# Score matmuls moved to the end of TensorE's attention step, with three moves on ScalarE and GpSimd that go with them

## The reference

```python
x = x + attn(layernorm(x))        # below
x = x + ffn(layernorm(x))         # top 4 of 32 experts per token, swiglu, plus a shared swiglu

def attn(X, Wq, Wv, q_norm_w, v_norm_w):
    K = X.reshape(B, L, H, d)
    Q = rms_norm_multihead((X @ Wq.T).reshape(B, L, H, d), q_norm_w)
    V = rms_norm_multihead((X @ Wv.T).reshape(B, L, H, d), v_norm_w)
    W = cumsum(einsum('blhd,blhe->blhde', K, V), axis=1)
    return einsum('blhd,blhde->blhe', Q, W).reshape(B, L, D)
```

## Time and profile before

| what | value |
|---|---|
| device time, median of 3 runs | 561.97 us (561.77 to 563.79) |
| profiled execution, its own time | 559.33 us |
| its span | 557.4 us |
| TensorE busy | 527.4 us (95%) |
| VectorE busy | 382.2 us (69%) |
| ScalarE busy | 376.5 us (68%) |
| GpSimd busy | 331.8 us (60%) |
| mean granted clock of TensorE | 0.983 |

### The profile page before, as it was taken

One profiled execution on the slowest core, in us unless ns is written; L12 is line 12 of the kernel. 1 busy time (PEld: TensorE's weight loads), 2 busy tenths in 40 slices (PEclk: granted clock), 3 DMA queues, 4 the chain that ended last, 5 costly groups with the idle time before them and its releaser, 6 DMA issues.

```text
span 557.4 us, 18176 instructions
## 1 busy us (share of the span) xinstructions
PE 527.4 (95%) x5177; PEld 383.1 (69%) x5177; DVE 382.2 (69%) x1354; ACT 376.5 (68%) x1258; POOL 331.8 (60%) x367
## 2 busy tenths in 40 slices
PE   6798999999999999699999999999999999997996
PEld 2355666666666665357998988999999995544554
DVE  7698999999999996664444444444444446744786
ACT  2687899988989985402766766777677776653452
POOL 6010377776777777771665555666666564446992
PEclk8999999999999999899999999999999999998999
DMA  8998355556456554954676776766666554428999
GB/s 259 316 292 264 125 217 211 187 215 227 186 198 246 188 192 152 366 194 127 195 219 201 221 225 199 214 193 194 194 193 198 180 187 145 143 79 342 408 409 347
DMA packets 65088, 123.29 MB, mean 221 GB/s; under 512 B 9824, under 2 KB 44000, under 8 KB 64992
## 3 DMA queue, kind: packets, MB, share of 16 engines
q1 hardware_dynamic: 47824, 78.07, 44.1%
q0 software_dynamic: 13056, 39.86, 19.2%
q10 hardware_dynamic: 4112, 4.19, 2.3%
HBM read 58.49 MB, written 63.60 MB: 219 GB/s over the span
## 4 chain that ended last, share of the span: by engine, by line
PE 79%; DMA 5%; DVE 4%; issue 4%; ACT 3%; POOL 2%; SPq 1%; ACTq 1%; DVEq 0%; POOLq 0%
PE pS L967 18%; PE pQV L828 10%; PE pS L985 9%; PE pS L741 8%; PE pS L795 5%; PE pO L888 5%; DMA xg<-xs 3%; PE pO L869 3%; PE pT L946 3%; PE pQV L946 2%; PE pQV L757 2%; PE pO L757 2%; PE pT L774 2%; PE pO L803 2%; PE pT L817 1%
## 5 line engine op out<-in xcount | busy, mean ns | idle before, releaser
L495 POOL DMA_INDIRECT ys<-gsh,dst x144 | 138.1, 959 | 108.3 <-ACT gsh L663 86.6
L467 POOL DMA_INDIRECT xs<-xg,posi x128 | 123.8, 967 | 52.1 <-issue 31.4
L967 PE MATMUL pS<-after_a,x2T_all 128*128 128x128 f32 x1024 | 135.5, 276 | 0.0
L967 PEld LDWEIGHTS pS<-after_a,x2T_all 128*128 128x128 f32 x1024 | 124.5, 192 | 0.0
L1375 DVE TENSOR_TENSOR after_a<-after_a,pS 128x128 f32<-128x128 f32 x144 | 41.5, 288 | 79.9 <-ACT after_a L651 76.1
L1346 DVE COPY x2T_all<-w 128x512 f32 x144 | 63.9, 444 | 32.9 <-issue 32.5
L985 PE MATMUL pS<-w,after_a 128*128 x256 | 76.7, 381 | 0.0
L1089 DVE TENSOR_TENSOR w<-pS,tri 128x512 f32<-128x512 f32 x96 | 65.1, 679 | 1.0 <-PE pS L795 1.0
L828 PE MATMUL pQV<-w 128*128 128x512 f32 x128 | 63.7, 621 | 0.5 <-ACT w L533 0.5
L663 ACT ACTIVATE gsh<-pS,xg 128x256 f32<-128x256 f32 x128 | 60.6, 474 | 0.4 <-issue 0.4
L662 ACT CAST dst<-xg 128x1 int32 x128 | 24.5, 191 | 45.3 <-PE pS L985 43.3
(11 more groups left out here) (221 smaller groups left out, 1019.8 us busy)
## 6 DMA issues: line engine op xcount, KB each, us to landing
xg<-xs SPq DMA_DIRECT2D x128, 160.0 KB, 2.8
ys<-gsh SPq DMA_DIRECT2D x32, 512.0 KB
w<-ys SPq DMA_DIRECT2D x32, 512.0 KB, 15.3
w<-in_L_ffn_W ACTq DMA_DIRECT2D x1, 4096.0 KB, 18.6
out<-xall SPq DMA_DIRECT2D x14, 256.0 KB, 7.2
xs<-padrow SPq DMA_DIRECT2D x32, 80.0 KB
xg<-xs SPq DMA_DIRECT2D x32, 80.0 KB, 2.2
ys<-gsh,dst POOLq DMA_INDIRECT x144
```

The lines of the kernel that those rows point to most:

```text
L467: pool.indirect_dma_start(out=xs, out_offset=bass.IndirectOffsetOnAxis(ap=posi[:, a.r8, k:k + 1], axis=0), in_=xr[:, a.r8, :], in_offset=N ...
L495: pool.indirect_dma_start(out=ys, out_offset=bass.IndirectOffsetOnAxis(ap=dst[:, j % 8:j % 8 + 1], axis=0), in_=y[:, j % 8, :], in_offset= ...
L967: last = pe.matmul(pS[a.b][:, n * P:(n + 1) * P], w13_staged(a.t)[:, (2 * k + n) * F:(2 * k + n + 1) * F], xgT[:, a.b, k, :], start=(k == ...
```

## The change

Four moves, no work added or removed. TensorE's scores of a tile go from the front of step t+2 (between L785 and L803) to the end of step t+1 (behind L888). ScalarE's copy of the scores goes to the front of its step. GpSimd's mask goes from behind the second scatter of a tile to behind the first. ScalarE's exponential for the Newton guess goes ahead of the router's L597.

```diff
@@ GpSimd
                     scatter(a, 0)
-                if (a := tile_of(9)) is not None:
-                    scatter(a, 1)
                 if (a := tile_of(2)) is not None:
                     pool_wait(S["s_copied"], banks_copied(a.t) + 1)
...
                                        pattern=[[0, 4], [1, P]], channel_multiplier=-1).then_inc(S["masked_pool"], 1)
+                if (a := tile_of(9)) is not None:
+                    scatter(a, 1)
@@ ScalarE
             def step(tile_of):
+                if (a := tile_of(3)) is not None:
+                    copy_scores(a, 1)
                 if (a := tile_of(1)) is not None:
                     wait(act, S["xnT_ps"], a.t + 1)
...
-                if (a := tile_of(3)) is not None:
-                    copy_scores(a, 1)
                 if (a := tile_of(2)) is not None:
                     wait(act, S["qT_ps"], a.t + 1)
...
-                if (a := closing(tile_of(7))) is not None:
-                    wait(act, S["max_done"], 2 * a.p + 2)
-                    act.activation(nmx[:, a.pb, :], m8[:, :, 0], ACT.Copy, scale=-1.0).then_inc(S["nmx_done"], 1)
                 if (a := tile_of(1, LAG)) is not None:
...
                     act.activation(guess[:, first:NR], lnm[:, first:NR], ACT.Exp, scale=-0.5).then_inc(S["guess_done"], 1)
+                if (a := closing(tile_of(7))) is not None:
+                    wait(act, S["max_done"], 2 * a.p + 2)
+                    act.activation(nmx[:, a.pb, :], m8[:, :, 0], ACT.Copy, scale=-1.0).then_inc(S["nmx_done"], 1)
@@ TensorE
-                if (a := tile_of(2)) is not None:
...
                     last.then_inc(S["o_ps"], 1)
+                if (a := tile_of(1)) is not None:
+                    if a.t == 0:
+                        pe.wait_ge(S["consts_dve"], DVE_CONSTS)
+                    wait(pe, S["qm_done"], a.t + 1)
+                    wait(pe, S["masked"], banks_masked(a.t))
+                    wait(pe, S["s_copied"], banks_copied(a.t))
+                    for g in range(KC):
+                        for j in range(4):
+                            last = pe.matmul(pS[j][:, g * 256:(g + 1) * 256], xnT[32 * j:32 * j + 32, a.r3, g, :],
+                                             qm[32 * j:32 * j + 32, :, g, :], start=(g == 0), stop=True,
+                                             skip_group_check=True)
+                            if g == KC - 1:
+                                last.then_inc(S["scores_ps"], 1)
```

## The result

The changed kernel takes 573.29 us (median of 4 runs, 572.57 to 575.17) where the kernel before took 562.36 beside it (4 runs, 561.77 to 563.79). The ratio is 1.0196, with a 95% interval of 1.0163 to 1.0229: slower, by about 2%.

The account below looks back on a forecast made before the run. Start-to-start waits on TensorE, with VectorE nearly full, left little to gain; a newly exposed ScalarE round trip would bind. Attention +10.6 and its edges +0.6 gave +11.2 on 561.97: 573.2 us, range 566.5 to 577.5.

Parts of the forecast that it names:

- The cover that goes: TensorE, attention: without the 1.08 us of scores, L817 (later L804) waits 0.63 us for ScalarE's copy L539 (later L541).
- The schedule of A: Attention step with L838 (before the change): forecast 6.51 us after the change, against 6.13 before.
- S: Time origin of an attention step: the moment when L888 has been issued, where L774 starts before the change.
- the floor: Attention, both step kinds: 2.07 us from L817 to L838 or L846, then the step's remaining pieces.
- The schedule of B: Attention step with L846 (before the change), softmax pieces ahead on ScalarE: forecast 6.58 us, against 6.07 before.
- the 10.6: Attention stretch of 25 steps: forecast loss of 10.6 us, counted as 0.85 us for each of 12.5 pairs.
- Waits that vanish: TensorE, attention: small waits, including 0.07 us at L828 and 0.15 at L888, paying back 0.3 to 0.35 a pair.
- Outside the stretch: First and last attention steps and stalled steps: +0.6 us in sum; the delay passes whole to the expert stage.
- The dearer round trip: Rival, attention: release takes 0.25 us instead of 0.15 and score copy 0.1 late; 577.0 us, chance 0.12.
- The clock: Rival, TensorE: waits in each step drop the granted clock to 1.2 GHz; over 600 us, chance 0.02.
- the round trip is hidden: Rival, attention: L817 does not in practice depend on this step's copies, so the change is faster; chance 0.06.
- The faster rival: Rival, attention: hidden round trip, pairs bounded by VectorE's 11.85 us, 4.4 to 4.9 us less, 557.3 us; chance 0.06.

Follow-up runs that it names:

- e5: Kernel before with only TensorE's scores moved to the end of the step; 25 attention steps 165.2 us (before: 153.0), whole-time ratio 1.0257.
- e9: Changed kernel with TensorE's output transposes ahead of the other two; 25 attention steps 175.9 us (changed kernel: 166.6), whole-time ratio to the kernel before 1.0428.
- e6: Changed kernel, guess and score copy at old places, transposed q in pT1 instead of pT0, waits adapted, output wrong; 25 attention steps 153.3 us, ratio 0.9995.
- e1: Changed kernel with ScalarE's L597 again ahead of the exponential for the Newton guess; 25 attention steps 164.4 us (changed kernel: 166.6), ratio 1.0198.
- e4: Kernel before with only GpSimd's mask moved one scatter earlier; 25 attention steps 152.4 us (before: 153.0), whole-time ratio 0.9976.
- e7: Kernel before with only ScalarE's exponential for the Newton guess ahead of L597; 25 attention steps 155.6 us (before: 153.0), whole-time ratio 1.0038.
- e2: Changed kernel with ScalarE's score copy back behind the copies of xnT and x2T; 25 attention steps 165.4 us (changed kernel: 166.6), ratio 1.0230.

## Why the prediction was right

573.2 was forecast, 573.29 measured. The mechanism was right, but a closeness of 0.1 us is luck. The profiled executions differ by 13.4 us (559.33 and 572.72) where 11.2 was forecast, and the median lies 0.6 above the profiled execution where 2.6 was taken over from the kernel before: two errors of about 2 us that cancel. By its steps:

**The cover that goes.** Right. The wait stands at L804, is ended by L541, in all 25 steps, and is 0.6 us long in the profile. e5 shows that TensorE's move alone brings it, e9 that taking away the rest of the cover makes it longer (0.78 us), e6 that without the shared bank it isn't there.

**The schedule of A.** L804 was put at S+2.57 and came at 2.51 (133.79 for 131.28): the release took 0.09, not 0.15. From there the floor was 3.94 us and the step took 4.01: L825 came at 2.10, not 2.07, and the piece behind it took 0.34, not 0.28. The sum, 6.51, met 6.52 by small errors of opposite sign. The 0.25 from the end of L562 to the router's matmul, which the floor uses, came again (135.64 to 135.89).

**The schedule of B.** Too small: 6.58 forecast, 6.81 to 6.88 in the steps at steady pace. L804 came at S+2.80 instead of 2.57. The prediction said of the score copy that it costs nothing, or up to 0.1 in B, and of the guess that it costs nothing. Both stand on ScalarE ahead of the copy that TensorE waits for. The prediction had the score copy released by the scores, at S+1.21, and ScalarE free at S+1.77. In B it started at S+1.58, behind the output copy, and ScalarE was free at S+2.04. (The 0.56 us read as the copy's own time was also the wait of L556 for L817; back to back it holds ScalarE 0.46.) With the copy in front, e1 puts 0.25 us of B's lateness at L804 on the guess. The step that failed is "in B, where the softmax pieces stand ahead, it may be up to 0.1 late", and the price of the guess: I looked for slack on VectorE, whom it serves, and not on ScalarE, where it runs. Over the stretch the longer B makes up the difference between the 10.6 and the 13.5.

**Waits that vanish.** Right: L815 starts 0.25 behind L804 and L875 0.58 behind L856, as where nothing holds them, and the only wait of TensorE's matmuls in the stretch is the one above. Start to start was the right reading of these waits: the time of both came back. The Trainium skill (Perfetto Trace Analysis, Identifying the Most-Contended Engine) warns against judging TensorE by its busy time. The trace agrees: waits of 0.07 and 0.15 us stood in a stretch where the row shows TensorE 99.5% busy. But the total doesn't decide it, since the busy row's 15.5 for the two waits lay nearer to the 13.5 us of the profile than my 10.6 did.

**Outside the stretch.** +0.6 forecast. Counting from the scores ahead of L774, the stretch begins 0.3 us later than before and what follows it, up to the expert blocks, takes 0.2 less, so +0.1. The standing still near 42 us didn't come back: TensorE is busy 5.44 of the 6 us from 40 to 46, and the rest is the wait of one L804. The delay went through whole.

**The rivals.** The dearer round trip (577.0) was nearest to what the profile shows, though not by a slower release (0.09 and 0.10) but by ScalarE's list in B. The clock stayed at 1.00. That the round trip is hidden is excluded by the bracket at L804. The faster rival was bounded at 0.35 us a pair by VectorE. That no more is won by taking one of TensorE's waits away agrees with e4 and e6 (152.4 and 153.3), but VectorE alone isn't shown to be the bound: in e6 its scaling of q ends last before the q transposes, in B of e4 ScalarE's copy does, 0.1 us behind VectorE.

The guess costs 2.6 us by itself in the order of before (e7), but nothing behind TensorE's move with the score copy at its old place (e2 beside e5). In e7 ScalarE's list had no room at L817. In e5 the q transposes wait for the round trip anyway, and in B L533 waits 0.29 us for L785; in e2 it still waits 0.21, so ScalarE's list comes in time in both. What stays open is the share of GpSimd's mask behind TensorE's move, which no version has alone there.

## What to carry to other kernels

Before a block of work is moved on an engine, ask what it stands between: here 1.08 us of matmuls, with 0.58 us of transposes around them, lay between a transpose and the overwriting of the bank from which another engine had to copy it, and covered a round trip of 1.16 us. Look for the waits behind the old place, not only for those at the new one. And price a reordering on the engine on which it happens, with all that is queued behind it, even if it is meant for another engine.

## What the runs showed that was not expected

- Two small instructions that depend on each other cost ScalarE more back to back here than with another between: the negated maximum and the exponential that reads it start 0.22 us apart (138.34, 138.56). With the guess between them (kernel before, 131.09 and 131.23), the exponential followed the instruction ahead of it after 0.14, and the maximum had filled a gap that was there anyway: logarithm and guess start 0.34 apart in both kernels.
- A copy's release of TensorE came 0.06 to 0.10 us behind the end of its record (L614 in e9, L541 in the changed kernel), less than the 0.15 of VectorE's L1240 and the 0.25 of ScalarE's L562 in the kernel before. The 0.25 stands in the changed kernel too, so the release isn't one figure but differs from place to place.
- TensorE's halt of 1.08 us near 42 us was there in the kernel before and not in the changed one, at the same share of the DMA engines (1.05). Its cause stays open. It isn't shown that the move took it away: e5, with the same order on TensorE, has a step of 7.17 us right behind (45.91 to 53.08), where the changed kernel has 6.69.
